# A decoder layer in float32: self attention in half-array tiles, routing logits with the gate as stationary operand

## Chip, cores, metric

The kernel runs on one core of a Trainium2 chip. The metric is device time in microseconds (us) of one execution; lower is better. The engines are TensorE (PE in the profile, its weight loads PEld), VectorE (DVE), ScalarE (ACT), GpSimd (POOL) and the DMA queue that SyncE issues (SPq).

## The reference

2048 tokens of 256 features (32 sequences of 64), float32. Three steps, each with residual and layer norm:

```python
# 1 self attention, linear, causal; LN after (q, k, v of xn = rms_norm(x))
q = silu(xn @ Wq.T); k = silu(xn @ Wk.T); v = silu(xn @ Wv.T); g = sigmoid(xn @ Wg.T)
o = causal_linear_attention(q, k, v) * g          # sum over j <= i of (q_i . k_j) v_j
x = layernorm(x + o @ Wp.T)
# 2 latent cross attention, 16 heads, rotary position, against ctx_512 (64 rows of 64 per sequence)
x = layernorm(x + softmax(q_r @ k_r.T) @ kv_r ... @ Wo.T)
# 3 experts: 32 of 96 inner features, top 8 by the softmax of the logits
logits = x @ gate_weight.T
combine = top-8 weights, renormalised, those under 0.05 dropped, renormalised again
x = layernorm(x + sum over e of combine[:, e] * ((silu(x @ Wg_e.T) * (x @ Wu_e.T)) @ Wd_e.T))
```

Causal attention never crosses a sequence of 64 tokens: of a 128-token tile's 128x128 scores only the two 64x64 squares on the diagonal count.

## The kernel before

Everything is split into four blocks of 512 tokens (four tiles of 128, eight sequences). Each engine has its own program, written out by hand, with semaphores between them; an engine runs its program strictly in order. `over_blocks` gives the order on every engine: `linear(0)` (self attention of block 0, with the folding of weights between), `pairs(0)`, and then for each block b `cross(b)` and `pairs(b+1)`, at last `cross(3)`, and the expert stage.

`pairs(b)` computes the queries of cross attention in 12 slots t, each of two halves k. A half is six matmuls `ps<-xT_hi,a_hi` and the like (lines 256 to 258, a float32 product split into three passes). VectorE turns each slot into four products with the rotary tables (line 1143) and GpSimd adds them (line 814). TensorE may start slot t when VectorE has read slot t-2. Between the slots TensorE does leftovers of the block before: transposes of x2 (`turn_x2`) in slots 0 and 1, and after slot 2 the routing logits of block b-1 (line 1499). VectorE reads these from PSUM at the end of its own slot 2 (`shift_logits`, lines 1249 and 1256), ScalarE takes Exp (line 923), and the rest of the routing (`route`) is spread over later slots.

`cross(b)` does cross attention of block b interleaved with self attention of block b+1. The stretch around the change is, on TensorE: `self_scores(n)` (line 1414), `context(2)` (line 1652), `self_context(n, 0)` and `(n, 1)` (line 1424), `xout(0)` (two transposes, line 1491), `turn(3)` (eight transposes, line 1635), `attn_out(n)` (line 1431). On VectorE: a `normalise`, `masked(n)` (line 1065), a `normalise`, `gated(n, 0)`, `gated(n, 1)` (line 1071), `norm2`, `residual1`. `attn_out` waits for both gatings. A plain float32 matmul appears in the trace as two matmul instructions, a transpose as one.

ScalarE's program at the start of `pairs(b)` matters for what follows. It copies the last two tiles of x2T, copies x1, then takes the square sums of the next block's x (`squares(b + 1)`, line 839, where there is a next block), and then Exp for the routing:

```python
            act.activation(x1[:], xn[:], ACT.Copy).then_inc(s_x1c, 1)
            if following:
                act.wait_ge(s_x1c, b + 1)
                squares(b + 1)
            if later:
                act.wait_ge(s_lsub, b)
                act.activation(rt[:, 1], rt[:, 0], ACT.Exp).then_inc(s_lexp, 1)
```

`squares` waits for the DMA of x. SyncE's queue issues that load (line 714, in `next_x`) behind the store of x2T of the block before (line 743, in `keep_x2`), which waits for the last of the x2T copies. The last block's logits are made in the first pass of the expert stage (`ffn_tensor`, step k = 5).

Of the kernel before, what the change touches and what calls it, by code (L numbers as in the profile page):

```python
# [28 lines left out]
ALU = mybir.AluOpType  # L29
# [32 lines left out]
def build(nc, a, out, c_dram):  # L62
# [18 lines left out]
    ropeq = sb(att, "ropeq", [P, 12, SEQ])  # L81
    sb(att, "spare", [P, 128])
    ropek = sb(att, "ropek", [P, 2, DC])
    mask = sb(att, "mask", [P, P])
    wp = sb(att, "wp", [P, KC, D])
# [88 lines left out]
    FIRST_KV_BANKS = (4, 5)  # L174
    LOGITS = ps[:, 7, 0:TILES * EXPERTS]
    m_bank = lambda g, h: 4 + (g + h) % 2
# [6 lines left out]
    a_psum = lambda k: ps[:, k % 4, 0:384].rearrange("p (r h c) -> p r h c", h=2, c=32)  # L183
    LAST_LOGITS = ps[:, 4, 0:TILES * EXPERTS]

# [31 lines left out]
    s_x2t, s_x2T = sem("x2T_in_psum"), sem("x2T_ready")  # L217
    s_lg = sem("logits_in_psum")
    s_lsub, s_lexp, s_c = sem("logits_shifted"), sem("logits_exp_ready"), sem("routing_ready")
# [165 lines left out]

    def ffn_scalar(act, x2T_out):
        def body(it, first, last):
            base = it * STEPS

            def hi(k):  # L390
                act.wait_ge(s_hc, base + k + 1)
                if not first or k >= 3:
                    act.wait_ge(s_d, base + k - 2)
                act.activation(h_hi[:, k % 3], hc[:, k % 2], ACT.Copy).then_inc(s_hhi, 1)  # L394

            for k in range(STEPS):
                act.wait_ge(s_g, base + k + 1)
                if not first or k >= 2:
                    act.wait_ge(s_su, base + k - 1)
                act.activation(sg[:, k % 2], bank(2 * (k % 2)), ACT.Silu).then_inc(s_sg, 1)  # L400
                if not first or k >= 1:
                    hi(k - 1)
                if first and k in X2_STEPS:
                    for i in range(2):
                        x2T_out(LAST, 2 * X2_STEPS.index(k) + i, 4 + i)
                if first and k == LOGITS_STEP + 2:
                    act.wait_ge(s_lsub, BLOCKS)
                    act.activation(rt[:, 1], rt[:, 0], ACT.Exp).then_inc(s_lexp, 1)
                if first and k == LOGITS_STEP:
                    y_hi_out(act, LAST)  # L410
                if first and k == TURN_C:
                    cT_out(act, LAST)

                part = k - f_hi_step(1, first, last)
                if 0 <= part < 3:
                    if part == 0:
                        act.wait_ge(s_fload[1], it * 32 + 32)
                    f_hi_out(act, 1, part)
                part = k - f_hi_step(0, first, last)
                if 0 <= part < 3 and not last:  # L420
                    if part == 0:
                        act.wait_ge(s_fload[0], it * 32 + 64)
                        act.wait_ge(s_d, base + (6 if first else 4) * ROWS)
                    f_hi_out(act, 0, part)
                if last and k in APPLY_STEPS:
                    final_apply(APPLY_STEPS.index(k))
            if last:
                hi(STEPS - 1)
                final_apply(2)
                final_apply(3)  # L430

        def final_apply(n):

            y = final_sum(n)
            act.wait_ge(s_scale, n + 1)
            for t in range(2 if n == LAST else TILES):
                act.activation(res[:, n, t], y[:, t], ACT.Identity, bias=fscale[:, n, 1, t:t + 1],
                               scale=fscale[:, n, 0, t:t + 1]).then_inc(s_res, 1)

        over_groups(act, body)  # L440
# [57 lines left out]
    def ffn_vector(dve, own, residual2, norm2, shift_logits, route):  # L498
# [22 lines left out]
        def body(it, first, last):  # L521
# [14 lines left out]
            for k in range(STEPS):  # L536
# [27 lines left out]
                if first and k == LOGITS_STEP + 1:  # L564
                    shift_logits(LAST, LAST_LOGITS)
                for part in range(6):
# [37 lines left out]

    def ffn_tensor(pe, turn_x2, logits):
        def body(it, first, last):
# [64 lines left out]
            for k in range(STEPS):  # L671
                if not first or k >= 2:
                    ffn_up(pe, it, k, first, last)
                    if last and k - 2 == TOKEN_STEPS[0]:
                        sum_turned()
                    if last and k - 2 in TOKEN_STEPS:
                        dn_tokens(k - 2)
                    else:
                        dn(k - 2)
# [5 lines left out]
                if first and k == LOGITS_STEP:  # L685
                    logits(LAST, LAST_LOGITS)
                if first and k == TURN_C:
# [147 lines left out]
    def _(act):  # L835
# [14 lines left out]
        def x2T_out(b, t, f):  # L850
            act.wait_ge(s_x2t, 4 * b + t + 1)
            if t == 0:
                act.wait_ge(s_kept, 32 * b + 1)
            act.activation(x2T[:, :, t * P:(t + 1) * P],
                           ps[:, f, 0:KC * P].rearrange("p (c s) -> p c s", c=KC), ACT.Copy).then_inc(s_x2T, 1)

        def bdT_out(b, i):
            act.wait_ge(s_bdt, 2 * b + i + 1)
# [53 lines left out]
        def pairs(b, later, following):  # L912
# [5 lines left out]
            if following:  # L918
                act.wait_ge(s_x1c, b + 1)
                squares(b + 1)  # L920
            if later:
                act.wait_ge(s_lsub, b)
                act.activation(rt[:, 1], rt[:, 0], ACT.Exp).then_inc(s_lexp, 1)
# [87 lines left out]
        over_blocks(linear, pairs, cross)  # L1011
        ffn_scalar(act, x2T_out)


    @block.vector
    def _(dve):
# [38 lines left out]
        def silu(b, i):  # L1055
# [4 lines left out]
                .then_inc(s_pa, 1)  # L1060

        def masked(b):

            dve.wait_ge(s_st, b + 1)
            dve.tensor_tensor(st[:].rearrange("p (t n) -> p t n", n=P), bank(6).rearrange("p (t n) -> p t n", n=P),
                              mask[:].unsqueeze(1).broadcast_to((P, TILES, P)), ALU.mult).then_inc(s_sm, 1)

        def gated(b, m):

            dve.wait_ge(s_ot, 2 * b + m + 1)  # L1070
            dve.scalar_tensor_tensor(out=gT[:, m], in0=gT[:, m], scalar=1.0, in1=bank((7, 6)[m]),
                                     op0=ALU.add, op1=ALU.mult).then_inc(s_og, 1)
# [66 lines left out]

        t64 = lambda ap: ap.rearrange("p (s n) -> p s n", n=SEQ)  # L1140

        def times(dst, src, table):
# [3 lines left out]
        def pairs(b, later, following):  # L1146

            def side(t, i):

                if later and t == 2 and i == 3:  # L1150
                    shift_logits(b - 1, LOGITS)
                if following and t == 4 and i == 3:
# [97 lines left out]

        def shift_logits(b, place):
            lg = place.rearrange("p (t x) -> p t x", x=EXPERTS)
            dve.wait_ge(s_lg, b + 1)
            red(row(0), lg, ALU.max)
            own.need()
            dve.tensor_tensor(r0, lg, rb(0), ALU.subtract).then_inc(s_lsub, 1)
# [121 lines left out]
    def _(pe):  # L1378
# [30 lines left out]
        def self_scores(b):  # L1409
            pe.wait_ge(s_th, 8 * b + 7)  # L1410
            for t in range(TILES):
                s = slice(t * P, (t + 1) * P)
                for kc in range(KC):
                    mm = pe.matmul(ps[:, 6, s], kT[:, kc, s], qT[:, kc, s], start=kc == 0, stop=kc == KC - 1)
            mm.then_inc(s_st, 1)

        def self_context(b, m):
            if m == 0:
                pe.wait_ge(s_th, 8 * b + 8)
                pe.wait_ge(s_pa, 6 * b + 6)  # L1420
                pe.wait_ge(s_sm, b + 1)
            for t in range(TILES):
                s = slice(t * P, (t + 1) * P)
                mm = pe.matmul(ps[:, 7 - m, s], v[:, t, m * P:(m + 1) * P], st[:, s], start=True, stop=True)
            mm.then_inc(s_ot, 1)
# [67 lines left out]

        def logits(b, place):

            pe.wait_ge(s_x2T, 4 * b + 4)
            for t in range(TILES):
                for kc in range(KC):
                    mm = pe.matmul(place[:, t * EXPERTS:(t + 1) * EXPERTS], x2T[:, kc, t * P:(t + 1) * P],
                                   gate_w[:, kc, :], start=kc == 0, stop=kc == KC - 1)  # L1500
            mm.then_inc(s_lg, 1)

# [5 lines left out]
        def linear(b):  # L1508
# [20 lines left out]
            fold_a(4, 8)  # L1529
            self_context(b, 0)  # L1530
            self_context(b, 1)
            fold_a(8, 10)
# [29 lines left out]
        def pairs(b, later, following):  # L1562
# [19 lines left out]
            for t in range(SLOTS):  # L1582
# [11 lines left out]
                for k in range(2):  # L1594
                    a = slice((2 * c + k) * P, (2 * c + k + 1) * P)
                    for kc in range(KC):
                        mm = split_matmuls(pe, bank(2 * (t % 2) + k), a_hi[:, kc, g, a], a_lo[:, kc, g, a],
                                           xT_hi[:, kc, :], xT_lo[:, kc, :], kc == 0, kc == KC - 1)
                    mm.then_inc(s_q, 1)
                if later and t == 0:  # L1600
                    pe.wait_ge(s_bdT, 2 * b + 2)
# [5 lines left out]
                if later and t == 2:  # L1607
                    logits(b - 1, LOGITS)
                if t in (4, 7, 10):
# [18 lines left out]
        def cross(b, following):  # L1628
# [42 lines left out]
            if following:  # L1671
# [20 lines left out]
                context(2)  # L1692
                self_context(n, 0)
                self_context(n, 1)
                xout(0)
# [42 lines left out]
        over_blocks(linear, pairs, cross)  # L1738
        ffn_tensor(pe, turn_x2, logits)

# [3 lines left out]
def _constants():  # L1744
# [3 lines left out]
    j, i = np.arange(P)[:, None], np.arange(P)[None, :]  # L1748
    c["mask"] = ((j // SEQ == i // SEQ) & (j <= i)).astype(f)

# [50 lines left out]
```

## Time and profile before

| | us |
|---|---|
| median of three runs | 854.82 (852.93 to 854.93) |
| profiled execution, its time | 853.3 |
| its span, first to last instruction | 851.3 |
| TensorE busy | 830.5 |
| VectorE busy | 634.7 |
| ScalarE busy | 280.0 |
| GpSimd busy | 182.2 |

The page shows one execution. Busy time of TensorE includes the tails of matmuls that overlap the next one, so the start of one group and the start of the next say more than the durations. Blocks 0 to 3 fill the first 459 us or so, the expert stage the rest.

### The profile page before, as it was taken

How to read it: one execution, taken by the hardware profiler on the slowest of the kernel's cores; microseconds unless marked ns; L12 is line 12 of the kernel's file. 1: busy time of each engine (PE TensorE's matmuls, PEld its weight loads, DVE VectorE, ACT ScalarE, POOL GpSimd, SP SyncE). 2: the span in 40 equal slices, each digit the busy share in tenths (PEclk: the TensorE clock that was granted, in tenths of full speed). 3: DMA queues.
4: the chain of work that ended last, by engine and by line, in shares of the span. 5: the costliest groups of instructions: out<-in, count | busy, mean ns of one | idle time of the engine just before them, and what ended most of it. 6: DMA issues, size and time to landing. Idle time of an engine off the chain costs nothing.

```text
span 851.3 us, 15983 instructions
## 1 busy us (share of the span) xinstructions
PE 830.5 (98%) x6348; PEld 669.0 (79%) x6348; DVE 634.7 (75%) x1392; ACT 280.0 (33%) x500; POOL 182.2 (21%) x152
## 2 busy tenths in 40 slices
PE   8999999999999999999899999999999999999996
PEld 7977678876887768876578888888888888888885
DVE  5687688899888998887867866657665666666576
ACT  5431353204432144301543423332323323232242
POOL 3046500563006620265511201200000000000121
PEclk9999999999999999999999999999999999999998
DMA  9300000100001000000320042201012020000001
GB/s 350 147 18 2 3 2 12 52 2 6 1 13 50 3 5 2 25 2 18 109 76 25 0 103 112 80 1 59 34 50 68 0 92 30 32 1 0 2 29 70
DMA packets 13091, 35.84 MB, mean 42 GB/s; under 512 B 1504, under 2 KB 2784, under 8 KB 12640
## 3 DMA queue, kind: packets, MB, share of 16 engines
q1 hardware_dynamic: 13024, 34.92, 11.9%
q8 instruction: 46, 0.75, 0.4%
q14 instruction: 21, 0.17, 0.1%
HBM read 30.26 MB, written 2.36 MB: 38 GB/s over the span
## 4 chain that ended last, share of the span: by engine, by line
PE 49%; DVE 2%; issue 1%; ACT 0%; POOL 0%; ACTq 0%; DVEq 0%
PE ps L256 15%; PE ps L257 15%; PE ps L258 14%; PE ps L1661 2%; PE ps L1652 1%; PE ps L639 1%; PE ps L1635 0%; PE ps L642 0%; PE ps L1557 0%; PE ps L667 0%; DVE h_lo L371 0%; PE ps L1506 0%; POOL roped L814 0%; DVE su L540 0%; PE ps L324 0%
## 5 line engine op out<-in xcount | busy, mean ns | idle before, releaser
L814 POOL TENSOR_TENSOR roped<-prod 128x512 f32<-128x512 f32 x96 | 121.3, 1290 | 231.2 <-DVE prod L1143 231.2
L540 DVE TENSOR_TENSOR su<-sg,ps 128x512 f32<-128x512 f32 x96 | 66.0, 687 | 120.4 <-PE ps L258 118.2
L256 PE MATMUL ps<-y_hi,f_hi 128*128 128x512 f32 x384 | 151.2, 394 | 0.0
L258 PE MATMUL ps<-y_hi,f_lo 128*128 128x512 f32 x384 | 149.5, 389 | 0.0
L257 PE MATMUL ps<-y_lo,f_hi 128*128 128x512 f32 x384 | 149.5, 389 | 0.0
L400 ACT ACTIVATE sg<-ps 128x512 f32<-128x512 f32 x96 | 57.3, 598 | 251.3 <-PE ps L258 251.2
L1143 DVE TENSOR_TENSOR prod<-ps,ropeq 128x512 f32<-128x512 f32 x192 | 118.7, 682 | 23.9 <-PE ps L258 21.6
L256 PEld LDWEIGHTS ps<-y_hi,f_hi 128*128 128x128 f32 x384 | 72.1, 188 | 15.2 <-issue 0.5
L258 PEld LDWEIGHTS ps<-y_hi,f_lo 128*128 128x128 f32 x384 | 72.1, 188 | 15.2
L257 PEld LDWEIGHTS ps<-y_lo,f_hi 128*128 128x128 f32 x384 | 72.1, 188 | 15.1 <-issue 0.5
L256 PE MATMUL ps<-xT_hi,a_hi 128*128 128x512 f32 x192 | 78.7, 410 | 2.1 <-DVE prod L1143 2.1
L546 DVE TENSOR_TENSOR hc<-su,cb 128x512 f32<-128x512 f32 x96 | 71.5, 744 | 6.0
L258 PE MATMUL ps<-xT_hi,a_lo 128*128 128x512 f32 x192 | 75.1, 391 | 0.0
L257 PE MATMUL ps<-xT_lo,a_hi 128*128 128x512 f32 x192 | 74.9, 390 | 0.0
L371 POOL TENSOR_TENSOR h_lo<-hc,h_hi 128x512 fp32r<-128x512 f32 x8 | 10.3, 1285 | 285.6 <-ACT h_hi L394 285.6
L256 PE MATMUL ps<-h_hi,f_hi 128*128 128x512 f32 x180 | 70.7, 393 | 0.6 <-DVE h_lo L371 0.4
L258 PE MATMUL ps<-h_hi,f_lo 128*128 128x512 f32 x180 | 70.1, 389 | 0.0
L257 PE MATMUL ps<-h_lo,f_hi 128*128 128x512 f32 x180 | 70.1, 389 | 0.0
L371 DVE TENSOR_TENSOR h_lo<-hc,h_hi 128x512 fp32r<-128x512 f32 x88 | 62.6, 712 | 0.1
L394 ACT ACTIVATE h_hi<-hc 128x512 fp32r<-128x512 f32 x96 | 59.9, 624 | 3.4 <-DVE hc L546 3.4
L909 ACT ACTIVATE lq<-ps 128x512 f32<-128x512 f32 x32 | 17.4, 596 | 127.7 <-PE ps L1576 127.7
L1661 PE MATMUL ps<-u_w,roped 128*128 128x256 f32 x256 | 57.9, 379 | 0.0
(186 smaller groups left out, 1348.0 us busy)
## 6 DMA issues: line engine op xcount, KB each, us to landing
cb<-routing SPq DMA_DIRECT2D x32, 256.0 KB
f_raw<-in_L_ffn_gate_up_proj SPq DMA_DIRECT2D x8, 768.0 KB, 6.2
f_raw<-in_L_ffn_down_proj SPq DMA_DIRECT2D x8, 384.0 KB, 7.1
xb<-in_x SPq DMA_DIRECT2D x4, 512.0 KB, 4.3
lq<-in_L_xattn_Wq SPq DMA_DIRECT2D x1, 2048.0 KB, 14.3
x2T_all<-in_L_xattn_Wo SPq DMA_DIRECT2D x1, 2048.0 KB, 11.9
x2T_all<-x2T SPq DMA_DIRECT2D x4, 512.0 KB, 3.3
roped<-in_L_xattn_w_kc_q SPq DMA_DIRECT2D x1, 1536.0 KB, 10.0
```

What stands on the lines that cost most here:

```text
L256: pe.matmul(dst, l_hi, r_hi, start=first, stop=False, skip_group_check=check)
L257: pe.matmul(dst, l_hi, r_lo, start=False, stop=False, skip_group_check=check)
L258: return pe.matmul(dst, l_lo, r_hi, start=False, stop=last, skip_group_check=check)
L371: eng.tensor_tensor(h_lo[:, k % 3], hc[:, k % 2], h_hi[:, k % 3].bitcast(F32), ALU.subtract).then_inc(s_hlo, 1)
L394: act.activation(h_hi[:, k % 3], hc[:, k % 2], ACT.Copy).then_inc(s_hhi, 1)
L400: act.activation(sg[:, k % 2], bank(2 * (k % 2)), ACT.Silu).then_inc(s_sg, 1)
L540: dve.tensor_tensor(su[:, k % 2], sg[:, k % 2], bank(2 * (k % 2) + 1), ALU.mult).then_inc(s_su, 1)
L546: dve.tensor_tensor(hc[:, k % 2], su[:, k % 2], cb[:, w, cols(n)], ALU.mult).then_inc(s_hc, 1)
L814: pool.tensor_tensor(roped[:, 2 * (t % 4) + k], made(2 * t + k)[:, 0], made(2 * t + k)[:, 1], ALU.add)\
L909: act.activation(lq[:, p].rearrange("p (h n) -> p h n", h=2), ps[:, f:f + 2, 0:256], ACT.Copy)\
L1143: return dve.tensor_tensor(t64(dst), t64(bank(src)), ropeq[:, table, :].unsqueeze(1).broadcast_to((P, SEQS, SEQ)), ALU.mult)
L1661: mm = pe.matmul(ps[:, f, 0:D], ct[:, c, :], u_w[:, (c + 4 * (t // 2)) % 8, :], start=c == 0, stop=c == PAIRS - 1)
```

## The change

Self attention by sequences. Scores: for each tile of 128 tokens and each half of the features, two matmuls instead of one, each with one sequence's 64 keys as stationary and its 64 queries as moving columns; the results of a tile's two sequences go to partitions 0 to 63 and 64 to 127 of the same 64 PSUM columns. The mask and the masked scores have 64 columns a tile instead of 128. Context: for each half of the features and each tile two matmuls, each over the 64 rows of one sequence, with 128 stationary columns of v and 64 moving columns; the two sequences of a tile go to banks 6 and 7. Both banks are signalled at once, after all 16 products (32 instructions), and VectorE's two gatings now go by bank, that is by sequence parity.

Logits. The gate's 32 columns are stationary, x2T moves, and the four tiles go to four groups of 32 partitions. ScalarE copies the 128x128 result to the routing buffer, TensorE transposes it, and VectorE reads the same layout as before. In `pairs` the products stand between the two halves of slot 2, the transpose behind the second half; in the expert stage the products stand between `ffn_up(5)` and the down product that follows, the transpose behind that.

```diff
-    mask = sb(att, "mask", [P, P])
+    mask = sb(att, "mask", [P, SEQ])
...
     def ffn_scalar(act, x2T_out, logits_out):
...
                 if first and k == LOGITS_STEP:
+                    logits_out(LAST)
                     y_hi_out(act, LAST)
...
     def ffn_tensor(pe, turn_x2, logits, turn_logits):
...
                     ffn_up(pe, it, k, first, last)
+                    if first and k == LOGITS_STEP:
+                        logits(LAST)
...
                 if first and k == LOGITS_STEP:
-                    logits(LAST, LAST_LOGITS)
+                    turn_logits(LAST)
...
+        def logits_out(b):
+            if b:
+                act.wait_ge(s_c, b)
+            act.wait_ge(s_lgr, b + 1)
+            act.activation(logits_rows, ps[:, logits_bank(b), P:2 * P], ACT.Copy).then_inc(s_lgc, 1)
...
                 squares(b + 1)
             if later:
+                logits_out(b - 1)
                 act.wait_ge(s_lsub, b)
                 act.activation(rt[:, 1], rt[:, 0], ACT.Exp).then_inc(s_lexp, 1)
...
-        def gated(b, m):
-            dve.wait_ge(s_ot, 2 * b + m + 1)
-            dve.scalar_tensor_tensor(out=gT[:, m], in0=gT[:, m], scalar=1.0, in1=bank((7, 6)[m]),
+        def gated(b, h):
+            dve.wait_ge(s_ot, b + 1)
+            g = gT[:, :, :].rearrange("p m (t h q) -> p (m t) h q", h=2, q=SEQ)[:, :, h]
+            dve.scalar_tensor_tensor(out=g, in0=g, scalar=1.0, in1=t64(bank(6 + h)),
                                      op0=ALU.add, op1=ALU.mult).then_inc(s_og, 1)
...
         def self_scores(b):
...
                 for kc in range(KC):
-                    mm = pe.matmul(ps[:, 6, s], kT[:, kc, s], qT[:, kc, s], start=kc == 0, stop=kc == KC - 1)
+                    for h in range(2):
+                        s = slice(t * P + h * SEQ, t * P + (h + 1) * SEQ)
+                        mm = pe.matmul(ps[64 * h:64 * h + 64, 6, t * SEQ:(t + 1) * SEQ], kT[:, kc, s], qT[:, kc, s],
+                                       start=kc == 0, stop=kc == KC - 1)
...
+            for m in range(KC):
+                for t in range(TILES):
+                    for h in range(2):
+                        r = slice(64 * h, 64 * h + 64)
+                        o = m * D + t * SEQ
+                        mm = pe.matmul(ps[:, 6 + h, o:o + SEQ], v[r, t, m * P:(m + 1) * P], st[r, t * SEQ:(t + 1) * SEQ],
+                                       start=True, stop=True)
...
+            for kc in range(KC):
+                for t in range(TILES):
+                    mm = pe.matmul(ps[32 * t:32 * t + 32, logits_bank(b), P:2 * P], gate_w[:, kc, :],
+                                   x2T[:, kc, t * P:(t + 1) * P], start=kc == 0, stop=kc == KC - 1)
+            mm.then_inc(s_lgr, 1)
+
+        def turn_logits(b):
+            pe.wait_ge(s_lgc, b + 1)
+            pe.transpose(logits_place(b), logits_rows, ident[:]).then_inc(s_lg, 1)
...
+                    if later and t == 2 and k == 0:
+                        logits(b - 1)
...
                 if later and t == 2:
-                    logits(b - 1, LOGITS)
+                    turn_logits(b - 1)
```

## Rows read from the trace of the kernel before

**Rows 1.** The page, part 1 and TensorE's granted clock in 40 slices (tenths).

```profile
PE 830.5 (98%) x6348; PEld 669.0 (79%) x6348; DVE 634.7 (75%) x1392; ACT 280.0 (33%) x500; POOL 182.2 (21%) x152
PEclk9999999999999999999999999999999999999998
```

**Rows 2.** Timeline of VectorE, slot 3; columns: start us, us, engine, line, operation, count, [idle before].

```profile
263.91 2.48 DVE L1143 TENSOR_TENSOR prod<-ps,ropeq 128x512 f32<-128x512 f32 x4 [1.55 <-PE ps L258]
```

**Rows 3.** Timeline of TensorE in cross attention of block 1.

```profile
229.42 1.95 PE L1414 MATMUL ps<-qkgv 128*128 128x128 f32 x16
231.20 1.88 PE L1652 MATMUL ps<-roped,bd 128*128 128x512 f32 x4
232.92 1.95 PE L1424 MATMUL ps<-st,qkgv 128*128 128x128 f32 x16
234.70 0.38 PE L1491 MATMUL ps<-ident,x 128*128 128x128 f32 x2
...
235.79 3.62 PE L1431 MATMUL ps<-wp,qkgv 128*128 128x256 f32 x16
```

**Rows 4.** Timeline of TensorE, slots 2 and 3, two blocks.

```profile
158.79 0.48 PE L256 MATMUL ps<-xT_hi,a_hi 128*128 128x512 f32 x1
...
257.48 0.39 PE L258 MATMUL ps<-xT_hi,a_lo 128*128 128x512 f32 x1
257.71 0.40 PE L256 MATMUL ps<-xT_hi,a_hi 128*128 128x512 f32 x1
...
259.09 1.86 PE L1499 MATMUL ps<-gate_w,x2T 128*128 128x32 f32 x16
260.79 0.48 PE L256 MATMUL ps<-xT_hi,a_hi 128*128 128x512 f32 x1
```

**Rows 5.** Timeline of TensorE where it works in small tiles (rows*columns).

```profile
17.00 0.87 PE L1456 MATMUL ps<-x2T_all 64*32 64x64 f32 x48
...
41.67 3.73 PE L1484 MATMUL ps<-x2T_all,prod 128*64 128x256 f32 x32
...
200.05 0.40 PE L258 MATMUL ps<-xT_hi,w_lo 128*128 128x512 f32 x1
200.37 0.46 PE L1557 MATMUL ps<-bdT,lq 64*64 64x64 f32 x16
200.76 0.50 PE L256 MATMUL ps<-xT_hi,w_hi 128*128 128x512 f32 x1
201.10 0.39 PE L257 MATMUL ps<-xT_lo,w_hi 128*128 128x512 f32 x1
```

**Rows 6.** The chain that ended last, in order: start us, us, what.

```profile
412.48 3.57 PE ps L1652 x4
416.05 1.09 PE ps L1557 x64
...
422.96 1.72 PE ps L1652 x4
```

**Rows 7.** Timeline of VectorE: the mask and the second gating, block 1.

```profile
231.52 0.69 DVE L1065 TENSOR_TENSOR st<-ps,mask 128x512 f32<-128x512 f32 x1
...
234.91 0.69 DVE L1071 SCALAR_TENSOR_TENSOR qkgv<-qkgv,ps 128x512 f32<-128x512 f32 x1 [0.21 <-PE ps L1424]
```

**Rows 8.** Timeline of the DMA queue: a load of x.

```profile
257.52 0.61 SPq L714 DMA_DIRECT2D xb<-in_x  x1
```

**Rows 9.** Timeline of ScalarE: squares and Exp, two blocks.

```profile
161.62 0.30 ACT L923 ACTIVATE rt<-rt 128x128 f32<-128x128 f32 x1
...
261.81 0.42 ACT L839 ACTIVATE xn<-xb 128x256 f32<-128x256 f32 x1 [3.93 <-DMA xb<-in_x]
...
263.42 0.30 ACT L923 ACTIVATE rt<-rt 128x128 f32<-128x128 f32 x1
```

**Rows 10.** Stretches: busy us (instructions) of PE, PEld, DVE, ACT, POOL, granted clock, DMA.

```profile
408.00:412.30 4.30, 1.33 (x12) 0.84 (x8) 4.20 (x7) 0.90 (x1) 0.55 (x1) 1.00 0.22 70
412.30:415.70 3.40, 3.22 (x4) 1.17 (x4) 2.89 (x6) 3.11 (x6) 2.47 (x3) 0.50 0.24 90
```

More of the change, by code:

```diff
@@ L81, in build @@
     ropeq = sb(att, "ropeq", [P, 12, SEQ])
-    sb(att, "spare", [P, 128])
+    sb(att, "spare", [P, 192])
     ropek = sb(att, "ropek", [P, 2, DC])
-    mask = sb(att, "mask", [P, P])
+    mask = sb(att, "mask", [P, SEQ])
     wp = sb(att, "wp", [P, KC, D])
@@ L174, in build @@
     FIRST_KV_BANKS = (4, 5)
-    LOGITS = ps[:, 7, 0:TILES * EXPERTS]
+    logits_bank = lambda b: 7 if b < BLOCKS - 1 else 4
+    logits_place = lambda b: ps[:, logits_bank(b), 0:TILES * EXPERTS]
+    logits_rows = rt[:, 2].rearrange("p t x -> p (t x)")
     m_bank = lambda g, h: 4 + (g + h) % 2
@@ L183, in build @@
     a_psum = lambda k: ps[:, k % 4, 0:384].rearrange("p (r h c) -> p r h c", h=2, c=32)
-    LAST_LOGITS = ps[:, 4, 0:TILES * EXPERTS]
     s_ident, s_tables = sem("ident_loaded"), sem("tables_loaded")
@@ L217, in build @@
     s_x2t, s_x2T = sem("x2T_in_psum"), sem("x2T_ready")
-    s_lg = sem("logits_in_psum")
+    s_lgr, s_lgc, s_lg = sem("logit_rows_in_psum"), sem("logit_rows_copied"), sem("logits_in_psum")
     s_lsub, s_lexp, s_c = sem("logits_shifted"), sem("logits_exp_ready"), sem("routing_ready")
@@ L384, in final_sum, with ffn_scalar @@
         return ps[:, f:f + 2, :].rearrange("p k (t d) -> p (k t) d", d=D)
-    def ffn_scalar(act, x2T_out):
+    def ffn_scalar(act, x2T_out, logits_out):
         def body(it, first, last):
@@ L564, in body @@
                 if first and k == LOGITS_STEP + 1:
-                    shift_logits(LAST, LAST_LOGITS)
+                    shift_logits(LAST)
                 for part in range(6):
@@ L603, in ffn_up, with ffn_tensor @@
             mm.then_inc(s, 1)
-    def ffn_tensor(pe, turn_x2, logits):
+    def ffn_tensor(pe, turn_x2, logits, turn_logits):
         def body(it, first, last):
@@ L1011, in _ @@
         over_blocks(linear, pairs, cross)
-        ffn_scalar(act, x2T_out)
+        ffn_scalar(act, x2T_out, logits_out)
     @block.vector
@@ L1060, in silu @@
                 .then_inc(s_pa, 1)
+        t64 = lambda ap: ap.rearrange("p (s n) -> p s n", n=SEQ)
         def masked(b):
             dve.wait_ge(s_st, b + 1)
-            dve.tensor_tensor(st[:].rearrange("p (t n) -> p t n", n=P), bank(6).rearrange("p (t n) -> p t n", n=P),
-                              mask[:].unsqueeze(1).broadcast_to((P, TILES, P)), ALU.mult).then_inc(s_sm, 1)
-        def gated(b, m):
-            dve.wait_ge(s_ot, 2 * b + m + 1)
-            dve.scalar_tensor_tensor(out=gT[:, m], in0=gT[:, m], scalar=1.0, in1=bank((7, 6)[m]),
+            dve.tensor_tensor(t64(st[:, 0:D]), t64(ps[:, 6, 0:D]), mask[:].unsqueeze(1).broadcast_to((P, TILES, SEQ)),
+                              ALU.mult).then_inc(s_sm, 1)
+        def gated(b, h):
+            dve.wait_ge(s_ot, b + 1)
+            g = gT[:, :, :].rearrange("p m (t h q) -> p (m t) h q", h=2, q=SEQ)[:, :, h]
+            dve.scalar_tensor_tensor(out=g, in0=g, scalar=1.0, in1=t64(bank(6 + h)),
                                      op0=ALU.add, op1=ALU.mult).then_inc(s_og, 1)
@@ L1138, in linear @@
             own.restart()
-        t64 = lambda ap: ap.rearrange("p (s n) -> p s n", n=SEQ)
         def times(dst, src, table):
@@ L1150, in side @@
                 if later and t == 2 and i == 3:
-                    shift_logits(b - 1, LOGITS)
+                    shift_logits(b - 1)
                 if following and t == 4 and i == 3:
@@ L1249, in red, with shift_logits @@
             own.step(dve.tensor_reduce(o, x, AX, op))
-        def shift_logits(b, place):
-            lg = place.rearrange("p (t x) -> p t x", x=EXPERTS)
+        def shift_logits(b):
+            lg = logits_place(b).rearrange("p (t x) -> p t x", x=EXPERTS)
             dve.wait_ge(s_lg, b + 1)
@@ L1411, in self_scores, with self_context @@
             for t in range(TILES):
-                s = slice(t * P, (t + 1) * P)
                 for kc in range(KC):
-                    mm = pe.matmul(ps[:, 6, s], kT[:, kc, s], qT[:, kc, s], start=kc == 0, stop=kc == KC - 1)
+                    for h in range(2):
+                        s = slice(t * P + h * SEQ, t * P + (h + 1) * SEQ)
+                        mm = pe.matmul(ps[64 * h:64 * h + 64, 6, t * SEQ:(t + 1) * SEQ], kT[:, kc, s], qT[:, kc, s],
+                                       start=kc == 0, stop=kc == KC - 1)
             mm.then_inc(s_st, 1)
[L1417 to L1424, printed above, removed]
+        def self_context(b):
+            pe.wait_ge(s_th, 8 * b + 8)
+            pe.wait_ge(s_pa, 6 * b + 6)
+            pe.wait_ge(s_sm, b + 1)
+            for m in range(KC):
[5 more added lines that the diff above has]
+                                       start=True, stop=True)
             mm.then_inc(s_ot, 1)
@@ L1492, in turn_x2, with logits @@
             mm.then_inc(s_x2t, 1)
-        def logits(b, place):
+        def logits(b):
             pe.wait_ge(s_x2T, 4 * b + 4)
[L1497 to L1501, printed above, removed]
+            for kc in range(KC):
[6 more added lines that the diff above has]
+            pe.transpose(logits_place(b), logits_rows, ident[:]).then_inc(s_lg, 1)
         def keep_warm(n, f=0):
@@ L1529, in linear @@
             fold_a(4, 8)
-            self_context(b, 0)
-            self_context(b, 1)
+            self_context(b)
             fold_a(8, 10)
@@ L1692, in cross @@
                 context(2)
-                self_context(n, 0)
-                self_context(n, 1)
+                self_context(n)
                 xout(0)
@@ L1738, in _ @@
         over_blocks(linear, pairs, cross)
-        ffn_tensor(pe, turn_x2, logits)
+        ffn_tensor(pe, turn_x2, logits, turn_logits)
     ctx.close()
@@ L1748, in _constants @@
     j, i = np.arange(P)[:, None], np.arange(P)[None, :]
-    c["mask"] = ((j // SEQ == i // SEQ) & (j <= i)).astype(f)
+    c["mask"] = (j % SEQ <= i[:, 0:SEQ]).astype(f)
     def table(dim):
```

## Prediction

> **What bounds the kernel now.** I read the page's first part, then TensorE's timeline where the changed steps stand, then what ScalarE and the DMA queue do there. TensorE is busy for 830.5 of 851.3 us, VectorE for 634.7, ScalarE for 280.0 [rows 1]. In the stretches that follow, one TensorE group starts where the one before it lets go, with VectorE waiting for it (1.55 us idle in [rows 2]). So TensorE's own time counts one for one, and so does each time that it is made to wait. The reader should also see how little TensorE's time depends on the moving columns: 16 instructions with 128 moving columns take 1.78 us (229.42 to 231.20 [rows 3]), 16 with only 32 take 1.70 us (259.09 to 260.79 [rows 4]). Both load 128 stationary columns each, so the load sets 0.11 us an instruction.
>
> **Prices of small tiles.** In the trace, 16 instructions of 64x64 take 0.39 us and 64 take 1.09 [rows 5, 6]. Four different tiles run together, so that is 4 and 16 rounds: (1.09 - 0.39) / 12 = 0.058 us a round, and 0.16 over for the start and the end. The change of tile shape costs twice more: the matmul before holds 0.32 instead of the usual 0.23 (200.05 to 200.37 against 257.48 to 257.71 [rows 4, 5]), and the first one after 0.34 (200.76 to 201.10), another 0.10. So a stretch of small tiles pays some 0.36 beside its rounds. Two column tiles of 128x64 do overlap: 32 instructions of 256 moving columns took 3.73 us to the end of the last, 16 rounds of 0.23 [rows 5]. One after another they would have needed 0.216 each (16 full-array matmuls of the same width, 235.79 to the end 3.62 later [rows 3]), 6.9 us. Four column positions of 32 do so too: 48 instructions took 0.87 us with the last one's tail, 12 rounds of about 0.06 [rows 5].
>
> **Self scores (four times).** 16 instructions of 128 columns become 32 of 64 stationary and 64 moving columns, in 16 rounds of two column tiles. By [rows 6] 16 rounds with their ends take 1.09, and with both shape changes 1.29: 1.78 - 1.29 saves 0.49 us of TensorE a block. The mask works on 256 columns instead of 512, so its 0.69 us [rows 7] becomes some 0.35; it is done while TensorE is in the 1.72 us of latent context either way, so that is worth nothing.
>
> **Self context (four times).** 16 instructions become 32 of 64 rows by 128 columns, in 16 rounds of two row tiles. No row shows this shape. From below, rounds of 0.058 as for 64 loaded columns: 0.93. From above, no overlap at all: 32 x 0.11 = 3.57. I take the loads of the two halves as running together but each as long as its 128 columns, 16 x 0.11 = 1.78 as before, because the 32-column and the 128-column rows take the same; with the shape changes +0.36. The Trainium skill (TensorEngine Tiling, Theoretical Speedup) promises up to twofold where a dimension is at most 64; the trace's load-bound rows say that halving the moving columns and the rows buys nothing while 128 columns are loaded. By that rule this step would fall by about 0.85 us before its shape changes.
>
> TensorE is then through self context 0.13 us earlier than before, at 234.57. But the gating changes its wait: before, the first gating started after half of the matmuls, and its second ended at 235.60 [rows 7], just before TensorE came for the output projection at 235.79 [rows 3]. Now both wait for all matmuls. Group end near 234.5, two gatings at some 0.69 each: 235.95. The 1.09 us of transposes behind self context (234.70 to 235.79) end at 235.66 and cover the rest. Output projection starts 0.15 to 0.2 later than before, in spite of the saved scores. Four blocks: **+0.8 us**. Ends: with rounds of 0.058 the gating chain still holds it at about 235.1, -0.7 a block, -2.8 in all; without overlap +2.0 a block, +8.
>
> **Logits, TensorE alone (four times).** 16 instructions at 1.70 become 4 rounds of four column tiles with 128 moving columns (0.11 each) and one transpose (0.11): 0.45 + 0.36 + 0.11, and with the changed shape of the one after some 0.9. Saving **0.85 us** each where nothing waits. That holds for the last block's logits in the expert stage (there the copy comes between a down product of six matmuls, 1.4 us, and nothing else is queued on ScalarE) and for the block before it, where ScalarE is idle: -1.7 us together.
>
> **Logits, the new wait (blocks 1 and 2 of the loop).** The transpose needs ScalarE's copy. In ScalarE's program the copy stands behind the square sums of the next block's x, and in front of Exp. Before, only Exp stood there, and nobody but routing waited for it. The squares wait for a DMA: x is issued at 257.52 [rows 8], behind the store of x2T in SyncE's program, and lands so that the first square starts at 261.81 and the last ends where Exp starts, 263.42 [rows 9]. TensorE's order is: first half of slot 2 (done 257.71), logits about 0.8, second half (1.38), transpose. It comes to the transpose at 259.9. The copy can run from 263.42 for some 0.3 (Exp of the same 128x128 takes 0.30 [rows 9]), so the transpose starts at 263.78 and slot 3 at 263.88. Before, slot 3 started at 260.79 [rows 4]: **+3.1 us**. One block earlier the squares are through at 161.62 [rows 9], slot 3 at 162.08 against 158.79 [rows 4]: **+3.3 us**. Queued behind the waiting transpose are all of slots 3 to 11; VectorE waits for them (it has 1.55 us of idleness there already [rows 2]) and GpSimd behind it. Nothing later has slack to give this back, since TensorE bounds the rest. The first pass has no logits, the last no squares.
>
> **The clock.** Beside the wait stands what it may do to TensorE's clock. Granted clock is 1.00 in all the long stretches; it falls to 0.50 (1.2 GHz) at 412.3 after a stretch in which TensorE was busy for 1.33 of 4.30 us [rows 10]. Four matmuls of 512 columns then took 3.57 us, later 1.72 [rows 6]: 1.85 us lost. The two new waits are 3.9 and 4.1 us with TensorE wholly idle, longer than any such wait of it in the rows. Ends: no fall (0), a fall after both (+3.7). I take one, **+1.85**.
>
> **Sum.** +0.8 - 1.7 + 3.1 + 3.3 = +5.5; with one fall of the clock +7.35. The profiled execution took 853.3 (span 851.3), so 860.7. It is 1.5 under the median of the runs shown, 854.82, which run from 852.93 to 854.93; I put the time at **861.0**.
>
> **Rivals.**
> - *No fall, or two.* 858.8 or 862.5 on the profiled execution. For two: the idle stretches are longer than the one in [rows 10] was. For none: it depends on where the idle time falls. The forecast case with 0, 1 or 2 falls has 0.20, 0.33 and 0.25.
> - *The wait is hidden, the change is faster.* If the square sums were over before TensorE is through slot 2, the copy would be free at once: x would have to land about 4 us earlier than it does. Then all four logits save 0.85: -3.4 + 0.8 = -2.6, 850.7. It decides at 259.9 in block 2: squares over by then, faster; later, each us is lost one for one. Against it: x cannot be issued before the last piece of x2T is copied, which the change does not move. 0.07.
> - *Row tiles do not overlap.* Self context costs +1.8 more a block, 7.2 in all: 868. For: no row shows 64x128. Against: 64x64 tiles in two row halves overlap. 0.08.
> - *Row tiles run at twice the rate.* -0.7 instead of +0.2 a block: -3.6 against the forecast, 857. 0.04.
> - *Column tiles that share rows do not hide their loads.* The trace's pairs of 128x64 streamed 256 columns, long enough to hide one load, so they do not prove it for 64. A round of self scores would be 0.11, the saving gone: +0.9 a block at most, 864. The Trainium skill (TensorE: Matmul & The Clock Gate, Part 3, The mechanism) says that a weight load overlaps running matmuls only when the row group differs, which speaks for this. The 64x64 rows, where tiles of the same rows and other columns keep rounds of 0.058, speak against. 0.03.
>
> **Range and chances.** About 0.3%, 2.6 us, is what can be told from no change. Left out below is the hidden wait (0.07) and some of the no-fall case, above the serial row tiles (0.08): 856.5 to 865.5. Faster by over 0.3%: 0.05 (part of the hidden wait). Within: 0.06. Slower: 0.89.
>
> **What would show it.** Two waits of TensorE for ScalarE's copy, each 3.5 to 4.5 us, in the second and third passes of the pairs, right after slot 2, and none in the fourth or the expert stage. ScalarE's copy directly behind the last square. Granted clock 0.50 in a stretch after a wait. Self scores at 1.1 to 1.3 us, self context at 1.8 to 2.1, output projection waiting for the second gating by 0.2 to 0.4. The prediction is wrong if the copy runs before the squares, if x lands earlier, or if self context's 32 instructions take over 3 us.

## The result

Measured: 862.06 us, median of four runs (861.69 to 863.16), against 853.93 (852.93 to 854.93) before, taken with it. The ratio is 1.0098, with a 95% interval of 1.0086 to 1.0110: 8.4 us slower (the two medians differ by 8.1). One execution of a later run, order_fix, took 2120 us where its other nine took 850.55 to 852.89, and its ratio leaves that one out. The profiled execution took 862.2, its span is 859.5, 8.2 more than before.

| | before | after |
|---|---|---|
| span | 851.3 | 859.5 |
| TensorE busy | 830.5 | 830.5 |
| VectorE busy | 634.7 | 633.6 |
| ScalarE busy | 280.0 | 281.2 |
| mean granted clock | 0.995 | 0.992 |

TensorE's busy time is the same in sum although the span grew. Work was saved, and matmuls at the lower clock put time back into the sum, while a wait lengthens the span alone. So the table doesn't show the cause; the longest waits do. From the list of waits of the changed kernel (engine, line, what it waited for: total us, times, longest):

```profile
PE ps L1523 <- ACT rt L865: 7.7, 2, 3.9
DVE rs L1261 <- PE ps L1523: 3.4, 2, 1.7
DVE xn L1090 <- PE ps L1449: 3.2, 5, 1.0
```

The first row didn't exist before: twice, TensorE waits 3.9 us for ScalarE's copy. TensorE's timeline around the second of them, in the columns of [rows 4], which it answers to:

```profile
262.70 0.39 PE L259 MATMUL ps<-xT_hi,a_lo 128*128 128x512 f32 x1
263.01 0.65 PE L1517 MATMUL ps<-x2T,gate_w 128*32 128x128 f32 x16
263.59 0.50 PE L257 MATMUL ps<-xT_hi,a_hi 128*128 128x512 f32 x1
...
264.85 0.39 PE L259 MATMUL ps<-xT_hi,a_lo 128*128 128x512 f32 x1
269.06 0.47 PE L1523 MATMUL ps<-ident,rt 128*128 128x128 f32 x1 [3.83 <-ACT rt L865]
269.19 0.77 PE L257 MATMUL ps<-xT_hi,a_hi 128*128 128x512 f32 x1
...
270.19 0.63 PE L259 MATMUL ps<-xT_hi,a_lo 128*128 128x512 f32 x1
270.62 0.63 PE L257 MATMUL ps<-xT_hi,a_hi 128*128 128x512 f32 x1
```

The logits themselves (line 1517) take 0.57 us where they took 1.70. Slot 2 is through at 265.08, and then nothing runs until 269.06. After that the matmuls of slot 3 start 0.43 apart instead of 0.23: the clock is down. ScalarE's side, the answer to [rows 9]:

```profile
261.61 0.39 ACT L858 ACTIVATE x2T<-ps 128x256 f32<-128x256 f32 x1 [2.52 <-PE ps L1509]
262.02 1.06 ACT L927 ACTIVATE x<-xn 128x1024 f32<-128x1024 f32 x1
267.14 0.42 ACT L843 ACTIVATE xn<-xb 128x256 f32<-128x256 f32 x1 [4.06 <-DMA xb<-in_x]
...
268.36 0.40 ACT L843 ACTIVATE xn<-xb 128x256 f32<-128x256 f32 x1
...
268.76 0.25 ACT L865 ACTIVATE rt<-ps 128x128 f32<-128x128 f32 x1
```

ScalarE is idle for 4.06 us before the squares, from 263.08 to 267.14. TensorE's wait begins at 265.2, so 1.9 us of it fall into this idle time and 1.6 into the squares. ScalarE could have made the copy (0.25 us) at 263.7, when the logits were through, but its program has the squares first, and these wait for x. The clock by stretches, columns as in [rows 10]:

```profile
157.00:162.80 5.80, 1.94 (x10) 1.29 (x9) 2.77 (x5) 1.87 (x9) 3.86 (x4) 1.00 0.45 142
162.90:166.20 3.30, 3.30 (x10) 2.52 (x9) 0.21 (x1) 0.31 (x1) 0.00 (x0) 0.50 0.02 5
264.00:268.60 4.60, 1.24 (x6) 0.68 (x4) 2.48 (x4) 1.46 (x7) 3.22 (x4) 1.00 0.54 175
268.70:272.00 3.30, 2.94 (x8) 2.36 (x9) 0.58 (x2) 0.62 (x4) 0.51 (x1) 0.50 0.00 0
```

It fell at both waits: at 162.8, 0.7 us after TensorE had begun to work again, and at 268.6, 0.4 us before it did. It was back at 1.00 from 166.2 and 272.1. And self attention in small tiles, TensorE's and VectorE's timeline, the answer to [rows 3] and [rows 7]:

```profile
234.50 1.15 PE L1427 MATMUL ps<-qkgv 128*64 128x64 f32 x32
235.58 1.98 PE L1675 MATMUL ps<-roped,bd 128*128 128x512 f32 x4
237.49 2.00 PE L1441 MATMUL ps<-st,qkgv 64*128 64x64 f32 x32
239.43 0.44 PE L1509 MATMUL ps<-ident,x 128*128 128x128 f32 x2
239.70 1.04 PE L1658 MATMUL ps<-ident,prod 128*128 128x128 f32 x8
240.88 3.72 PE L1449 MATMUL ps<-wp,qkgv 128*128 128x256 f32 x16
```
```profile
239.54 1.28 DVE L1085 SCALAR_TENSOR_TENSOR qkgv<-qkgv,ps 128x512 f32<-128x512 f32 x2 [1.06 <-PE ps L1441]
```

From start to start the scores take 1.08 us (1.78 before), the context 1.94 (1.78). The two gatings start together at 239.54, end at 240.82, and the output projection follows at 240.88. From the start of the scores to that of the output projection it is 6.38 us, as before (229.42 to 235.79, 6.37 [rows 3]). Of this the last 0.31 us are a wait for the gatings: the eight transposes before the output projection (line 1658) need 0.87 from start to start and have 1.18. Another 0.1 lies ahead of the scores, where the tile shape changes (line 1684 to the scores 3.55 us, 3.46 before), and 0.1 in the output projection (3.56 to the group behind it, 3.46 before).

### The profile page after: what moved, and what is told of

Same layout as the page of the kernel before. It is cut to its first block, busy times and chain, and to the rows that moved or that the text cites. A ratio compares the mean times of both kernels' runs of the same rounds, so it can differ in the third digit from the quotient of the medians.

```text
span 859.5 us, 16254 instructions
## 1 busy us (share of the span) xinstructions
PE 830.5 (97%) x6480; PEld 661.8 (77%) x6480; DVE 633.6 (74%) x1392; ACT 281.2 (33%) x504; POOL 181.3 (21%) x152
## 4 chain that ended last, share of the span: by engine, by line
PE 49%; DVE 2%; issue 1%; ACT 0%; POOL 0%; ACTq 0%; DVEq 0%
PE ps L257 15%; PE ps L258 14%; PE ps L259 14%; PE ps L1684 2%; PE ps L1675 1%; PE ps L641 1%; PE ps L1658 0%; PE ps L1578 0%; PE ps L644 0%; PE ps L669 0%; DVE h_lo L372 0%; PE ps L1528 0%; POOL roped L818 0%; DVE su L542 0%; PE ps L325 0%
```

## Experiments

The theory: the loss is the two waits behind the square sums and what they do to the clock, and without them the change would be a small gain. Rivals: the small tiles themselves cost the time; or ScalarE's squares as work, not their wait for x. Times in us are for a kernel before of 854.1, by the ratio measured beside it.

**order_fix.** ScalarE's copy moved ahead of the squares.

```diff
             act.activation(x1[:], xn[:], ACT.Copy).then_inc(s_x1c, 1)
+            if later:
+                logits_out(b - 1)
             if following:
                 act.wait_ge(s_x1c, b + 1)
                 squares(b + 1)
             if later:
-                logits_out(b - 1)
                 act.wait_ge(s_lsub, b)
```

> The changed kernel with one edit: ScalarE makes the copy of the logits before the square sums of the next x, not after them. Theory (the transpose waits for a copy queued behind squares that wait for x, and the clock falls in that wait): both waits of 4.0 us and both falls of the clock (1.7 and 1.4 us) go, which leaves the cheaper logits, 4 x -0.88, and the self attention, 4 x +0.2: 2.7 us under the kernel before, about 851.2 where that has 853.9. Rival (the small tiles themselves or the new transpose cost the time, the wait only shows it): within 2 us of the changed kernel, 860 to 862.

Measured: ratio 0.9969 (0.9959 to 0.9979), 2.6 us under the kernel before. TensorE and ScalarE at the same place:

```profile
257.67 0.64 PE L1518 MATMUL ps<-x2T,gate_w 128*32 128x128 f32 x16
...
259.53 0.40 PE L259 MATMUL ps<-xT_hi,a_lo 128*128 128x512 f32 x1
259.76 0.27 PE L1524 MATMUL ps<-ident,rt 128*128 128x128 f32 x1
259.79 0.47 PE L257 MATMUL ps<-xT_hi,a_hi 128*128 128x512 f32 x1
```
```profile
256.28 0.38 ACT L858 ACTIVATE x2T<-ps 128x256 f32<-128x256 f32 x1 [2.54 <-PE ps L1510]
...
258.44 0.28 ACT L865 ACTIVATE rt<-ps 128x128 f32<-128x128 f32 x1 [0.69 <-PE ps L1518]
262.05 0.42 ACT L843 ACTIVATE xn<-xb 128x256 f32<-128x256 f32 x1 [3.33 <-DMA xb<-in_x]
```

The copy runs in the gap in which ScalarE waits anyway, and the transpose follows slot 2 without a wait. The place of one instruction in ScalarE's program is worth 11 us (1.0098 against 0.9969). The rival, 860 to 862, falls. From the last x2T copy to the start of slot 3 it is 3.51 us (256.28 to 259.79), against 7.58 in the changed kernel (261.61 to 269.19).

**x_early.** Nothing moved on ScalarE; the DMA of x is issued ahead of the store of x2T.

```diff
-            keep_x2(b)
             if b + 1 < LAST:
                 next_x(b + 1)
+            keep_x2(b)
             keep_c(b)
```

> The changed kernel with the order of the DMA queue changed instead: x of the next block is loaded ahead of the store of x2T, so that it has long landed when ScalarE comes to the squares; the copy stays behind the squares. Theory: the squares then run right behind the copy of x1, some 4 us earlier, and are over at about the time at which TensorE is through slot 2: the waits shrink from 4.0 us to under 0.3 each, no fall of the clock, 851 to 852. Rival (it is the position behind the squares as such, 1.6 us of ScalarE's work, that costs): waits of 1.5 us or more remain, 855 or more.

Measured: ratio 0.9973 (0.9963 to 0.9983), 2.3 us under the kernel before. The squares start right behind the copy of x1 and the copy of the logits just in time:

```profile
257.58 0.42 ACT L843 ACTIVATE xn<-xb 128x256 f32<-128x256 f32 x1
...
258.80 0.40 ACT L843 ACTIVATE xn<-xb 128x256 f32<-128x256 f32 x1
...
259.20 0.25 ACT L865 ACTIVATE rt<-ps 128x128 f32<-128x128 f32 x1
```
```profile
259.32 0.39 PE L259 MATMUL ps<-xT_hi,a_lo 128*128 128x512 f32 x1
259.55 0.29 PE L1523 MATMUL ps<-ident,rt 128*128 128x128 f32 x1
```

The load of x for these squares is now issued at 247.48, 9 us ahead of the store of x2T (256.49); in the changed kernel it is issued at 262.71, right behind that store (262.02), which waits for x2T's last tile. In this run as in order_fix TensorE never waits for the copy, and its clock stays at 1.00 in these passes. So it is not the squares as work that cost, but the load for which they wait.

**warm_wait.** The wait stays and is filled with products that nobody uses.

```diff
                 if later and t == 2:
+                    if following:
+                        keep_warm(9, 6)
                     turn_logits(b - 1)
```

> The changed kernel with nine warming products (256 columns, float32, 0.43 us each) put into TensorE's program ahead of the transpose in the two passes that wait; they fill the wait of 4.0 us and compute nothing that is used. Theory: the wait stays as long as it is, but the clock doesn't fall: 3.1 us under the changed kernel, about 859, and granted clock 1.00 in slots 3 and 4. Rival (the clock falls for another reason, or its fall is hidden by VectorE): no change, 862.

Measured: ratio 1.0061 (1.0044 to 1.0078), 5.2 us over the kernel before where the changed one has 8.4 over. The 18 instructions fill the time from 263.87 to the transpose at 267.99, and the granted clock stays at 1.00 behind them:

```profile
262.00:266.00 4.00, 4.00 (x32) 3.31 (x25) 2.53 (x6) 0.00 (x0) 2.65 (x3) 1.00 0.80 262
266.00:272.00 6.00, 5.92 (x27) 4.68 (x26) 2.01 (x6) 2.18 (x10) 2.01 (x2) 1.00 0.00 1
```

In this pass the copy ends at 267.94 and the transpose follows at 267.99, so the products don't hold it up. The clock's part of the loss is some 3 us by the ratios, 2.4 by the spans (857.1 against 859.5), and the wait alone is the rest. Pass by pass, from the output projection of one block to that of the next (blocks 1 to 2, 2 to 3), in us:

| | 1 to 2 | 2 to 3 |
|---|---|---|
| no wait (order_fix) | 101.43 | 101.47 |
| wait, clock kept (warm_wait) | 105.56 | 105.52 |
| wait and fall (changed kernel) | 106.96 | 106.72 |

A wait by itself costs 4.1 us, and its fall of the clock 1.4 and 1.2.

**old_self.** The changed kernel with self attention as before.

```diff
-            self_context(b)
+            self_context(b, 0)
+            self_context(b, 1)
```
(and with it `self_scores`, `masked`, `gated` and the mask as before, at both places.)

> The changed kernel with self attention as before (full-array tiles, mask of 128 columns, two signals), the logits as changed. Theory: the saved scores and the dearer context with its single signal are worth +0.2 us a block, so taking them back gives -0.8: about 861.3, with both waits of 4.0 us still there. Rival (self attention in small tiles carries a large part of the loss, 1.8 us a block or more): 855 or less.

Measured: ratio 1.0096 (1.0079 to 1.0114). The rival with 1.8 us a block falls. Whether it is the 0.8 us of the theory can't be told from these times: the difference to the changed kernel is 0.2 us, with intervals of 1 to 1.5 us on each side.

**old_logits.** The other half alone: the kernel before with the changed self attention, logits as before. (The edit is the change without its logits.)

```diff
-            self_context(b, 0)
-            self_context(b, 1)
+            self_context(b)
```

> The kernel before with the changed self attention alone; logits as before. Theory: +0.2 us a block, +0.8 in all, 854.7 where the kernel before has 853.9; scores 0.5 us shorter, context 0.2 to 0.4 longer, and the output projection waits for the second gating. Rival (the saved scores come through): -2.0, 852.

Measured: ratio 1.0012 (1.0003 to 1.0020), +1.0 us (+0.3 to +1.7). The saved scores don't come through; self attention in half-array tiles is a small loss. The spans of the two profiled executions, both with a mean clock of 0.995, differ by 0.7 us (852.0 against 851.3).

**fix_old_self.** The reverse: only the logits as changed, with the copy ahead of the squares.

```diff
+            if later:
+                logits_out(b - 1)
...
-                logits_out(b - 1)
```
(The copy as in order_fix, self attention as in old_self.)

> Logits as changed with ScalarE's copy ahead of the squares, self attention as before. Theory: only the four cheaper logits are left, 4 x -0.88 = -3.5 us against the kernel before, 850.4 where that has 853.9, and 0.8 under the kernel with the copy moved and the new self attention. Rival (self attention in small tiles gains): 852 or more.

Measured: ratio 0.9961 (0.9948 to 0.9974), -3.3 us. That is the four logits at 0.83 each. It is 0.7 under order_fix, which agrees with old_logits, though the intervals of the two overlap. The traces tell it more closely: from the output projection of block 1 to that of block 2 it is 101.21 us here and 101.43 in order_fix, from block 2 to block 3 101.18 and 101.47, so the new self attention costs 0.2 to 0.3 us a block.

**fix_quarter.** The copy ahead of the squares, and self context cut once more, into tiles of 64x64.

```diff
-                        mm = pe.matmul(ps[:, 6 + h, o:o + SEQ], v[r, t, m * P:(m + 1) * P], st[r, t * SEQ:(t + 1) * SEQ],
-                                       start=True, stop=True)
+                        for c in range(2):
+                            q = slice(64 * c, 64 * c + 64)
+                            mm = pe.matmul(ps[q, 6 + h, o:o + SEQ], v[r, t, m * P + 64 * c:m * P + 64 * c + 64],
+                                           st[r, t * SEQ:(t + 1) * SEQ], start=True, stop=True)
```

> The copy ahead of the squares, and self context in tiles of 64x64 instead of 64x128: 64 instructions that load 64 columns each, four tiles at a time, 16 rounds. Theory (a round of small tiles is as long as its load, 0.11 us for 128 columns and 0.058 for 64): the group falls from 1.93 to about 1.1 us, and the output projection starts 0.75 us earlier a block: 3.0 us under the kernel with only the copy moved, about 848.5. Rival (the rounds are bound by the number of instructions or by rows): no gain, or a loss up to 3 us.

Measured: 847.55 us, ratio 0.9922 (0.9909 to 0.9935), 6.7 us under the kernel before and 4.0 under order_fix.

TensorE's timeline in cross attention of block 1, the same place as above:

```profile
227.39 1.15 PE L1428 MATMUL ps<-qkgv 128*64 128x64 f32 x32
228.47 1.98 PE L1678 MATMUL ps<-roped,bd 128*128 128x512 f32 x4
230.38 1.16 PE L1444 MATMUL ps<-st,qkgv 64*64 64x64 f32 x64
231.48 0.44 PE L1512 MATMUL ps<-ident,x 128*128 128x128 f32 x2
231.75 1.04 PE L1661 MATMUL ps<-ident,prod 128*128 128x128 f32 x8
232.95 3.72 PE L1452 MATMUL ps<-wp,qkgv 128*128 128x256 f32 x16 [0.17 <-DVE qkgv L1086]
```

Twice as many instructions take 1.10 us instead of 1.94. From the scores to the output projection it is 5.56 us instead of 6.38. That is 0.82 a block, 3.3 in all; the measured difference is 0.7 larger. The five executions of fix_quarter have mean clocks of 0.995 to 0.998 and spans of 845.4 to 845.8; of order_fix's nine, five have 0.995 or 0.996 and spans of 848.8 to 848.9, the other four 0.993 or 0.994 and 850.3 to 850.9. At like clocks the difference is 3.0 to 3.5 us, so the 0.7 more lies in the clock and not in the tiles. Of all kernels here this is the fastest. What bounds it there is again the gating: the output projection comes only when both gatings are through (0.17 us of it shown as a wait).

## Why the prediction was right

861.0 was forecast, 862.06 measured, and the causes are those on record. The nearness of the number owes something to luck: one fall of the clock at 1.85 us was put where two at 1.4 and 1.2 came, and the two errors nearly cancel. Of the three clock cases the one that came, two falls, had been given 0.25, less than the 0.33 for one.

- *The new wait.* Forecast +3.1 and +3.3 us for slot 3. Measured by the distance from the last x2T copy to the start of slot 3, in the second pass 154.64 to 162.21, in the third 261.61 to 269.19, against 154.43 to 158.79 and 256.41 to 260.79 before: +3.2 and +3.2. TensorE's two waits are 3.9 and 3.8 us (3.9 and 4.1 forecast), and the copy starts where the last square ends (268.76). order_fix and x_early, two edits on different engines with nothing in common but the time at which the copy can run, both took the waits away and gave the same time. That is what shows the cause, and not only where the time went.
- *The logits by themselves.* Forecast 0.85 each, though the prediction's own terms, 0.45 + 0.36 + 0.11 against 1.70, give 0.78; order_fix has 3.51 us from x2T copy to slot 3 where the kernel before had 4.38, so 0.87. fix_old_self gives 0.83 for each of four. Column tiles of 32 that share their rows do run four at a time: the 16 instructions take 0.57 us, and in the trace they start in fours, 0.007 us apart, with 0.11 to 0.13 from four to four. The scores' 32 instructions took 1.08 us (forecast 1.09), in pairs 0.058 apart; with loads that are not hidden the rival had 0.11 for such a round. The rule weighed as a rival, that loads overlap running matmuls only across row groups (the Trainium skill, TensorE: Matmul & The Clock Gate, Part 3, The mechanism), does not hold for these two shapes.
- *Self context.* The forecast took the round to be as long as its load of 128 columns. The group took 1.94 us: its 16 pairs, the two of a pair 0.007 us apart, follow each other at 0.11, which makes the 1.78 of the forecast, and 0.16 is left for the start and the end, as was put. fix_quarter then halved the loaded columns, with rows and moving columns as they were, and the group fell to 1.10, in rounds of 0.058. So both ends of the range, 0.93 and 3.57, were away from it, and time was saved only when the loaded columns, too, were 64. The twofold speedup that the Trainium skill (TensorEngine Tiling, Theoretical Speedup) allows to a dimension of 64 did not come with 64 rows alone.
- *The gating.* Forecast: both gatings behind all matmuls hold the output projection 0.15 to 0.2 us later, in sum with the scores. By itself it came out even (6.38 us from the scores on, 6.37 before), with 0.31 of wait, and 0.2 lies beside the stretch, in the matmuls ahead of the scores and in the output projection. So the 0.2 a block was right in sum, less so in its place. For the four blocks +0.8 was forecast, and old_logits gives +1.0. What block 0 gave can't be told: the output projection of block 1 starts between 133.81 and 134.52 us in the traces other than fix_quarter's, and in fix_old_self, with the old self attention, it starts latest.
- *The clock: the term that was mis-sized.* One fall was taken, with 1.85 us; there were two, at 1.4 and 1.2 (the changed kernel against warm_wait). So the term was 1.85 where 2.6 came. Both its parts were off. The number of falls was a choice between none, one and two. The price was read from [rows 6]: 3.57 against 1.72 us for the same four matmuls.

  TensorE waits for VectorE soon after these (0.71 us in the second row below), so most of that loss is given back. In old_self the clock did not fall at that place. From the start of the four matmuls to the first product of line 1678 (its u_w products) it is 6.20 us there, and to the expert stage 19.71. In the changed kernel, where it fell as it did before the change, it is 6.88 and 19.85. Behind the four matmuls and the 64 of line 1578 the loss is 1.6 us (4.61 against 3.01 from the start); 0.7 of it reached those products, and 0.14 the expert stage. In the slots nothing gives the time back: two stretches of 3.4 us at the lower clock, with the matmuls 0.43 instead of 0.23 us apart, lose the 1.4 and 1.2. Of the second, 0.4 us fell into the wait, which fits its smaller loss.

First of these two, in old_self, then the changed kernel, TensorE's timeline:

```profile
421.49 1.98 PE L1669 MATMUL ps<-roped,bd 128*128 128x512 f32 x4 [1.11 <-ACT roped L953]
...
427.20 0.66 PE L1652 MATMUL ps<-ident,prod 128*128 128x128 f32 x4 [0.71 <-DVE prod L1210]
427.69 1.03 PE L1678 MATMUL ps<-u_w,roped 128*128 128x256 f32 x4
...
441.20 0.79 PE L257 MATMUL ps<-y_hi,f_hi 128*128 128x512 f32 x1
```
```profile
421.55 3.14 PE L1675 MATMUL ps<-roped,bd 128*128 128x512 f32 x4 [1.11 <-ACT roped L953]
...
428.43 0.38 PE L1684 MATMUL ps<-u_w,roped 128*128 128x256 f32 x1
...
441.40 0.79 PE L257 MATMUL ps<-y_hi,f_hi 128*128 128x512 f32 x1
```

A longer fall at this place is not given back. In fix_old_self the clock was down from 409.3 to 416.1, 6.8 us where the changed kernel has 3.4 here, and it is 20.85 us to the expert stage, 1.1 more than without a fall:

```profile
410.97 3.78 PE L1670 MATMUL ps<-roped,bd 128*128 128x512 f32 x4 [1.11 <-ACT roped L954]
...
431.82 0.80 PE L257 MATMUL ps<-y_hi,f_hi 128*128 128x512 f32 x1
```

With the terms as measured the sum is 3.2 + 3.2 + 2.6 + 0.8 - 1.7 = 8.1, against 8.2 in the spans.

What stays open: how often the clock falls after such a wait. It fell after both in the profiled execution, and the four timed runs had a mean clock of 0.990 to 0.992, old_self too shows two falls after these waits. No run here has a wait of this length with the clock kept, except the one filled with work, so a chance for it can't be given.

## What to carry to other kernels

When a step is given to another engine for a moment, read what stands ahead of it in that engine's program and what that waits for, back to the DMA; a copy of 0.25 us cost 11 us here, 8 of waiting and the rest by the clock, because it stood behind squares that waited for a load. A round of small matmuls was as long here as the longer of its load and its stream (0.11 us with 128 columns loaded and 64 moving, or with 32 loaded and 128 moving; 0.058 with 64 and 64), so halving the moving columns was worth something only where the stationary ones were halved with them. Price a fall of the clock where it will happen: beside a wait for another engine 3.4 us at half the clock cost 0.14 us, and a fall twice as long 1.1; in a stretch bound by TensorE 3.4 us of it cost 1.4.

## What the runs showed that was not expected

Two tiles of 64x128 in different row halves run together, each round as long as one load (0.11 us), and tiles of 64x64 four at a time in rounds of 0.058, although two and two of the four (the column halves) write to the same bank. 64 instructions of the small shape are faster than 32 of the large one and than the 16 of the kernel before. And x_early showed that a load of 512 KB moved to 9 us ahead of the store cost nothing that can be measured: x_early and order_fix differ by 0.3 us, within their intervals.
